# An RWKV attention and mixture-of-experts layer on one core: the last columns of each expert's gate and up packed into two full tiles, and the expert's steps reordered

## Chip, core and metric

The kernel runs on one core of one Trainium2 chip. A core has five engines that run their own instruction streams and meet at semaphores: TensorE (PE in the profile, its weight loads as PEld), VectorE (DVE), ScalarE (ACT), GpSimd (POOL) and SyncE (SP, which here only issues DMAs). The metric is the device time of one execution in microseconds (us), the median over the runs. Lower is better.

## What is computed

The layer takes x of shape (8, 512, 512), normalizes it, and adds an attention branch and a feed-forward branch to it. The change touches only the routed experts of the feed-forward branch, cut here to what matters:

```python
E, K, F = (32, 4, 352)          # experts, experts per token, hidden width
CAP = 256                       # rows of one expert
x = w_norm * (xf * rsqrt(mean(xf * xf) + eps))       # 4096 tokens, H = 512
probs = softmax(x @ w_router); w_topk, sel = top_k(probs, K)
buf = the rows of x sent to each expert, at most CAP   # (E, CAP, H)
g = einsum('ech,ehf->ecf', buf, w_gate)
u = einsum('ech,ehf->ecf', buf, w_up)
y = einsum('ecf,efh->ech', silu(g) * u, w_down)
out = y gathered back, weighted by w_topk, plus a shared expert
```

Everything is float32. The kernel reaches that precision on TensorE by splitting each operand into a high part (rounded to the format fp32r) and a low part (the rest), and adding three products: low weight with high row, high weight with low row, high with high (`PRODUCTS`).

## The kernel before

Three stages follow one another: the projections of the attention (`project_stage`, to about 430 us), the 32 experts (`expert_stage`, about 435 to 870 us) and the output stage (`output_stage`: shared expert, attention output, final sums). The change is inside the second.

**One expert** has 256 rows of 512 channels (KC = 4 chunks of 128). The hidden width of 352 is cut into three tiles `FT` of 128, 128 and 96 columns. On TensorE `one_expert` runs, for each tile, 12 gate products and 12 up products (3 part pairs x 4 chunks, line 1400), each with up to 128 weight columns held in the array and the 256 rows streamed: 72 products. Then `turn` (line 1392) transposes the 256 gathered rows of the next expert in 8 steps, and `down` (line 1427) makes 18 products of 512 columns.

**Around TensorE**, for each tile: ScalarE takes silu of the gate out of PSUM (`silu`, line 1256), VectorE multiplies it by up (`hidden`, line 1339), ScalarE rounds the result to its high part (`hidden_hi`, line 1262), VectorE makes the low part (`hidden_lo`, line 1344), and `down` waits for that (`h_lo`). Of the next expert, prepared meanwhile: ScalarE makes the high parts of the gate, up and down weights (`gate_hi` line 1234, `up_hi` line 1238, `down_hi` lines 1242 and 1244) and of the turned rows (`rows_hi`, line 1250). VectorE makes the low parts of up, down and rows (`up_lo` 1318, `down_lo` 1324 and 1326, `rows_lo` 1333). GpSimd makes the low part of the gate weights (`gate_lo`, line 1210) and issues the indirect DMAs that gather the rows of the expert after the next (line 1201). `keep_y` (line 1269) copies the expert's output out of PSUM. SyncE loads the weights two experts ahead.

Each engine's order is the order of the calls in its own `one_expert`; no scheduler changes it. An instruction that waits holds back all that stands behind it on its engine. Weights, inputs, rows and outputs have two buffers (`half`), `act_g` and `h` have one. Each tile has a PSUM bank of its own, gate in its first half and up in its second (`gu`).

## Time and profile before

| | us |
|---|---|
| median of 3 runs | 1688.76 |
| lowest and highest | 1687.11, 1691.56 |
| the profiled execution, device time | 1695.61 |
| its span, first to last instruction | 1693.8 |

The rows below come from the profiled execution, which is 6.85 us longer than the median. The page gives busy times and the chain of work that ended last, followed back from the end. A timeline lists the instructions of an engine by their start, like ones merged ("x12"), with the idle time before them in brackets. The busy time of a merged row runs to the end of its last instruction. Matmuls overlap: each is listed with 282 ns, while the next starts 118 ns later, so the pace is read from the starts of rows.

### The profile page before, as it was taken

To read this page: it belongs to the slowest core of one execution; us is meant where nothing else is said; L and a number is where in the kernel's file an instruction comes from. 1 tells how busy PE (TensorE), PEld (TensorE's weight loads), DVE (VectorE), ACT (ScalarE), POOL (GpSimd) and SP (SyncE) were. 2 spreads that over 40 slices of the span, in tenths; PEclk is the share of its full clock that TensorE was granted. 3 is DMA by queue.
4 is the path that set the end of the run, shared out by engine and by line. 5 is a ranking of instruction groups with operands and counts; after the bars stand their busy time and mean duration, and the time that the engine had idled before them with its cause. 6 is when DMAs were issued, how large, how long until landed. Compare 5 with 4: busy or idle time off the path is not lost.

```text
span 1693.8 us, 26093 instructions
## 1 busy us (share of the span) xinstructions
PE 1647.0 (97%) x8512; PEld 1402.2 (83%) x8512; DVE 1272.6 (75%) x1863; ACT 697.7 (41%) x1216; POOL 836.7 (49%) x691
## 2 busy tenths in 40 slices
PE   6999999998999999999998999999999999999999
PEld 4777888876999999999986788888788888888887
DVE  7989999997756555655579687676777768687776
ACT  5746555653766666666653212121221212112121
POOL 4587777774444444444457444251433525243351
PEclk9999999999999999999999999999999999999999
DMA  4544343424766666666687655454545343433431
GB/s 156 194 155 174 125 156 141 149 100 181 253 240 244 239 241 234 228 228 230 239 278 230 234 176 162 174 182 148 179 143 178 104 155 119 155 107 114 166 99 52
DMA packets 122420, 299.06 MB, mean 177 GB/s; under 512 B 19996, under 2 KB 31260, under 8 KB 117728
## 3 DMA queue, kind: packets, MB, share of 16 engines
q1 hardware_dynamic: 103104, 263.82, 43.6%
q0 software_dynamic: 18944, 33.66, 6.9%
q8 instruction: 44, 0.72, 0.2%
q10 hardware_dynamic: 288, 0.52, 0.1%
q14 instruction: 40, 0.33, 0.1%
HBM read 233.34 MB, written 81.35 MB: 186 GB/s over the span
## 4 chain that ended last, share of the span: by engine, by line
PE 74%; DVE 15%; issue 6%; ACT 2%; POOL 2%; another core or an unknown queue 0%; DMA 0%; DVEq 0%; POOLq 0%; ACTq 0%; SPq 0%
PE bank L2176 25%; PE bank L1400 16%; PE bank L2190 13%; PE bank L1427 8%; PE bank L2207 5%; PE bank L1024 4%; DVE mixf L719 3%; PE bank L1392 2%; DVE bank L687 1%; DVE st L667 1%; DVE mix L726 1%; DVE zT_lo L694 1%; DVE s_wg L2027 1%; PE bank L958 1%; DVE sr L740 1%
## 5 line engine op out<-in xcount | busy, mean ns | idle before, releaser
L1024 PE MATMUL bank<-mix,w 128*128 128x512 f32 x1488 | 353.7, 394 | 12.8 <-DVE ekv L735 7.6
L1024 PEld LDWEIGHTS bank<-mix,w 128*128 128x128 f32 x1488 | 277.0, 189 | 76.3 <-DVE ekv L735 5.8
L2176 PE MATMUL bank<-s_zT,s_wu 128*128 128x512 f32 x1056 | 256.7, 392 | 9.9 <-DVE bank L1932 9.9
L2190 PE MATMUL bank<-s_wd,s_h 128*128 128x512 f32 x1056 | 254.0, 390 | 1.1 <-DVE s_h L1938 1.1
L2176 PE MATMUL bank<-s_zT,s_wg 128*128 128x512 f32 x1056 | 253.7, 389 | 0.0
L2176 PEld LDWEIGHTS bank<-s_zT,s_wu 128*128 128x128 f32 x1056 | 199.5, 189 | 53.4 <-issue 11.9
L2190 PEld LDWEIGHTS bank<-s_wd,s_h 128*128 128x128 f32 x1056 | 198.4, 188 | 42.9 <-DVE s_h L1938 1.7
L2176 PEld LDWEIGHTS bank<-s_zT,s_wg 128*128 128x128 f32 x1056 | 198.2, 188 | 41.1
L1210 POOL TENSOR_TENSOR e_wg<-e_g_in,e_wg 128x1408 fp32r<-128x1408 f32 x31 | 100.7, 3249 | 212.6 <-ACT e_wg L1234 212.6
L1707 POOL DMA_INDIRECT s_picked<-y_rows,s_slot x128 | 140.6, 1099 | 78.3 <-DVE s_total L1988 39.1
L1816 ACT ACTIVATE s_act_g<-bank 128x512 f32<-128x512 f32 x88 | 52.5, 597 | 288.6 <-PE bank L2176 282.2
L1827 ACT ACTIVATE s_h<-bank 128x512 fp32r<-128x512 f32 x80 | 47.9, 598 | 263.5 <-DVE bank L1932 260.4
L1400 PE MATMUL bank<-e_xT,e_wu 128*128 128x256 f32 (+1 forms) x1152 | 152.1, 282 | 0.0
L1400 PE MATMUL bank<-e_xT,e_wg 128*128 128x256 f32 (+1 forms) x1152 | 152.1, 282 | 0.0
L1400 PEld LDWEIGHTS bank<-e_xT,e_wg 128*128 128x128 f32 (+1 forms) x1152 | 144.3, 180 | 2.6
L374 POOL TENSOR_TENSOR mix<-mixf,mix 128x512 fp32r<-128x512 f32 x88 | 118.4, 1358 | 50.3 <-ACT mix L498 49.3
L1400 PEld LDWEIGHTS bank<-e_xT,e_wu 128*128 128x128 f32 (+1 forms) x1152 | 142.1, 180 | 0.0
L1427 PE MATMUL bank<-e_wd,e_h 128*128 128x512 f32 (+1 forms) x576 | 140.1, 396 | 0.0
L1988 DVE SCALAR_TENSOR_TENSOR s_total<-s_picked,s_rec,s_total 128x512 f32<-128x512 f32 x128 | 136.9, 1070 | 3.4
L388 POOL DMA_INDIRECT slot_tokens<-token,slot x112 | 119.3, 1065 | 33.9 <-issue 24.3
L1427 PEld LDWEIGHTS bank<-e_wd,e_h 128*128 128x128 f32 (+1 forms) x576 | 106.2, 189 | 21.4
L1727 POOL TENSOR_TENSOR s_att<-s_gate,s_att 128x512 fp32r<-128x512 f32 x32 | 46.2, 1445 | 156.7 <-ACT s_att L1845 156.7
(188 smaller groups left out, 2489.3 us busy)
## 6 DMA issues: line engine op xcount, KB each, us to landing
s_wu<-wu_split SPq DMA_DIRECT2D x77, 512.0 KB
e_g_in<-in_w_gate SPq DMA_DIRECT2D x32, 704.0 KB
e_u_in<-in_w_up SPq DMA_DIRECT2D x32, 704.0 KB
e_d_in<-in_w_down SPq DMA_DIRECT2D x32, 512.0 KB
y_rows<-e_y SPq DMA_DIRECT2D x32, 512.0 KB, 2.9
s_zT<-zT_parts SPq DMA_DIRECT2D x16, 1024.0 KB, 6.8
zT_parts<-zT_hi SPq DMA_DIRECT2D x8, 1024.0 KB
zT_parts<-zT_lo SPq DMA_DIRECT2D x8, 1024.0 KB
```

What stands on the lines that cost most here:

```text
L374: pool.tensor_tensor(mix[:, i % 2, k, 1, :], mixf[:, k, :], mix[:, i % 2, k, 0, :].bitcast(F32), ALU.subtract).then_inc(lo_made, 1)
L388: pool.indirect_dma_start(d["slots"], bass.IndirectOffsetOnAxis(ap=slot[:, half, at:at + 1], axis=0), token[:, half, at // TOPK:at // TOPK ...
L1024: last = pe.matmul(pj[m][:], w[i][:, w_part, k, m * P:(m + 1) * P], mix[:, i % 2, k, x_part, :], start=(k == 0 and q == 0), stop=(k == KC ...
L1210: pool.tensor_tensor(wg[half][:, 1, :], g_in[half][:], wg[half][:, 0, :].bitcast(F32), ALU.subtract).then_inc(wg_lo, 1)
L1400: last = pe.matmul(gu[f][0:m, which, :], w[half][:, w_part, k * F + f0:k * F + f0 + m], xT[half][:, x_part, k, :], start=(q == 0 and k == ...
L1427: last = pe.matmul(yp[c][:], h[0:m, f, h_part, c * P:(c + 1) * P], wd[half][0:m, w_part, f, :], start=(f == 0 and q == 0), stop=(f == NF - ...
L1707: pool.indirect_dma_start(picked[:, k, :], None, d["y_flat"], bass.IndirectOffsetOnAxis(ap=slot[:, j * TOPK + k:j * TOPK + k + 1], axis=0) ...
L1816: act.activation(act_g[:, i, :], gp[:], ACT.Silu).then_inc(silu_made, 1)
L1988: dve.scalar_tensor_tensor(total[:, j, :], picked[:, k, :], rec[:, at:at + 1], total[:, j, :], ALU.mult, ALU.add).then_inc(picked_used, 1)
L2176: last = pe.matmul(into[:], w[:, w_part, k, :], zT[:, x_part, k, :], start=(q == 0 and k == 0), stop=(q == 2 and k == KC - 1))
L2190: last = pe.matmul(yp[j][:], h[:, i, h_part, j * P:(j + 1) * P], wd[f][:, w_part, :], start=(f == 0 and q == 0), stop=(f == NFS - 1 and q ...
L2207: last = pe.matmul(ob[j % 2][:], att[m][:, x_part, j * P:(j + 1) * P], wo[m][:, w_part, :], start=(m == 0 and q == 0), stop=(m == KC - 1 a ...
```

## The change

**Packing.** Gate and up together have 704 columns, which is five and a half tiles of 128, but took six (two of them with 96 columns). Now the gate weights are loaded as `w_first`, 384 columns wide: the 352 of gate and behind them the last 32 of up. The third gate tile so has 128 columns (96 gate, 32 up) and still 12 products. Of up remain 256 columns in two whole tiles, and 64 columns (`UA`), whose high and low parts lie side by side in one tile of 128 columns (`wua`). That tile takes 4 products with the low rows and 4 with the high rows, 8 in place of 12 (`product_third`). An expert has 68 products. The host lays the two weight arrays out (`w_first`, `w_second`); their bytes are together the same as before.

**Putting it together.** The up values of the third tile now come in three pieces of bank 6. ScalarE copies two of them to an SBUF tile `third` (`keep_third`, two instructions), VectorE adds the third piece (one more instruction), and the multiplication of the third tile then takes both of its inputs from SBUF (`act_g` and `third`).

**Order.** The packed tile is the first of an expert, then tiles 0 and 1 (`ORDER`). TensorE turns the next rows between its second and last tile. ScalarE does `up_hi` of the next expert at the start and `gate_hi` after the first tile's silu and `keep_third` (before: `gate_hi` at the start, `up_hi` after the first silu); `rows_hi` stands ahead of the last tile's silu. VectorE does `up_lo` ahead of the first `hidden`, and `rows_lo` ahead of the last. `up_hi` and `up_lo` are two instructions each (256 and 1024 elements a row, before one of 1408). `gate_hi` and `gate_lo` have 1536 elements a row, before 1408.

```diff
-        def silu(e, f):
+        def silu(e, at):
+            f = ORDER[at]
...
+        def keep_third(e):
+            act.wait_ge(up_done, e * NF + 1)
+            wait(act, h_made, gated(e - 1, 0) if not isinstance(e, int) or e else 0)
+            act.activation(third[0:UA, :], gu[2][UA:2 * UA, 1, :], ACT.Copy)
+            act.activation(third[UA:UA + UB, :], gu[2][P - UB:P, 0, :], ACT.Copy).then_inc(silu_made, 1)
...
             if more:
+                up_hi(e + 1, 1 - half, other)
+            silu(e, 0)
+            keep_third(e)
+            if more:
                 gate_hi(e + 1, 1 - half, other)
-            silu(e, 0)
-            if more:
-                up_hi(e + 1, 1 - half, other)
...
-        def hidden(e, f):
+        def hidden(e, at):
+            f = ORDER[at]
             m = FT[f][1]
-            dve.wait_ge(silu_made, e * NF + f + 1)
-            dve.tensor_tensor(act_g[0:m, f, :], act_g[0:m, f, :], gu[f][0:m, 1, :], ALU.mult).then_inc(h_made, 1)
+            dve.wait_ge(silu_made, gated(e, at))
+            if at == 0:
+                dve.tensor_tensor(third[0:UA, :], third[0:UA, :], gu[f][0:UA, 1, :], ALU.add).then_inc(h_made, 1)
+                dve.wait_ge(h_made, e * GATES + 1)
+            up = gu[f][0:m, 1, :] if at else third[0:m, :]
+            dve.tensor_tensor(act_g[0:m, f, :], act_g[0:m, f, :], up, ALU.mult).then_inc(h_made, 1)
...
+        def product_third(half):
+            for x_part in (1, 0):
+                for k in range(KC):
+                    last = pe.matmul(gu[NF - 1][:, 1, :], wua[half][:, k].rearrange("p q f -> p (q f)"),
+                                     xT[half][:, x_part, k, :], start=(x_part == 1 and k == 0),
+                                     stop=(x_part == 0 and k == KC - 1))
+            return last
...
         def one_expert(e, half, more, uses):
-            for f in range(NF):
-                up_gate(e, half, f)
+            up_gate(e, half, 0)
+            up_gate(e, half, 1)
             if more:
                 turn(e + 1, 1 - half, uses + half)
+            up_gate(e, half, 2)
             down(e, half)
```

ScalarE in the last but one expert, before, from the high part of the gate weights to the first of the turned rows (`e_wg1`, `e_wu1` are the next expert's weights, `e_act_g` takes silu, `e_h` the rounded hidden values):

```order
L1234 ACTIVATE e_wg1_120<-e_g_in1_126 128x1408 [waits e_y_done,e_g_loaded1]
L1256 ACTIVATE e_act_g_135<-bank6 128x256 [waits e_h_lo,e_up_done]
L1238 ACTIVATE e_wu1_122<-e_u_in1_128 128x1408 [waits e_u_loaded1]
L1262 ACTIVATE e_h_136<-e_act_g_135 128x256 [waits e_y_done,e_h_made]
L1256 ACTIVATE e_act_g_135<-bank0 128x256 [waits e_h_lo,e_up_done]
L1262 ACTIVATE e_h_136<-e_act_g_135 128x256 [waits e_y_done,e_h_made]
L1256 ACTIVATE e_act_g_135<-bank1 96x256 [waits e_h_lo,e_up_done]
L1262 ACTIVATE e_h_136<-e_act_g_135 96x256 [waits e_y_done,e_h_made]
L1250 ACTIVATE e_xT1_134<-bank4,keep_const_51 128x256 [waits e_turned]
```

And now, in the same place:

```order
L1256 ACTIVATE e_wua1_124<-e_u_in1_130 128x4x64 [waits e_y_done,e_u_loaded1]
L1257 ACTIVATE e_wu1_122<-e_u_in1_130 128x1024
L1276 ACTIVATE e_act_g_137<-bank6 96x256 [waits e_h_lo,e_up_done]
L1282 ACTIVATE e_third_139<-bank6 64x256 [waits e_h_made,e_up_done]
L1283 ACTIVATE e_third_139<-bank6 32x256
L1251 ACTIVATE e_wg1_120<-e_g_in1_128 128x1536 [waits e_y_done,e_g_loaded1]
L1290 ACTIVATE e_h_138<-e_act_g_137 96x256 [waits e_y_done,e_h_made]
L1276 ACTIVATE e_act_g_137<-bank0 128x256 [waits e_h_lo,e_up_done]
L1290 ACTIVATE e_h_138<-e_act_g_137 128x256 [waits e_y_done,e_h_made]
L1269 ACTIVATE e_xT1_136<-bank4,keep_const_51 128x256 [waits e_turned]
```

The conversion of the gate weights (`e_wg1`), which releases GpSimd, stood ahead of the first silu. Now it stands directly ahead of the first rounding of hidden values (`e_h`). The turned rows (line 1269, four instructions) moved ahead of the last silu, which follows them.

VectorE in the same expert, before (the first row multiplies silu by up, `e_h` rows make low parts, `e_xT1` rows the low parts of the next rows):

```order
L1339 TENSOR_TENSOR e_act_g_135<-e_act_g_135,bank6 128x256 [waits e_silu_made]
L1318 TENSOR_TENSOR e_wu1_122<-e_u_in1_128,e_wu1_122 128x1408 [waits e_wu_hi]
L1344 TENSOR_TENSOR e_h_136<-e_act_g_135,e_h_136 128x256 [waits e_h_hi]
L1339 TENSOR_TENSOR e_act_g_135<-e_act_g_135,bank0 128x256 [waits e_silu_made]
L1344 TENSOR_TENSOR e_h_136<-e_act_g_135,e_h_136 128x256 [waits e_h_hi]
L1339 TENSOR_TENSOR e_act_g_135<-e_act_g_135,bank1 96x256 [waits e_silu_made]
L1344 TENSOR_TENSOR e_h_136<-e_act_g_135,e_h_136 96x256 [waits e_h_hi]
L1333 SCALAR_TENSOR_TENSOR e_xT1_134<-bank4,keep_const_51,e_xT1_134 128x256 [waits e_x_hi] x2
L1333 SCALAR_TENSOR_TENSOR e_xT1_134<-bank5,keep_const_51,e_xT1_134 128x256 [waits e_x_hi] x2
```

And now:

```order
L1348 TENSOR_TENSOR e_wua1_124<-e_u_in1_130,e_wua1_124 128x4x64 [waits e_wu_hi]
L1349 TENSOR_TENSOR e_wu1_122<-e_u_in1_130,e_wu1_122 128x1024
L1372 TENSOR_TENSOR e_third_139<-e_third_139,bank6 64x256 [waits e_silu_made]
L1375 TENSOR_TENSOR e_act_g_137<-e_act_g_137,e_third_139 96x256 [waits e_h_made]
L1381 TENSOR_TENSOR e_h_138<-e_act_g_137,e_h_138 96x256 [waits e_h_hi]
L1375 TENSOR_TENSOR e_act_g_137<-e_act_g_137,bank0 128x256 [waits e_silu_made]
L1381 TENSOR_TENSOR e_h_138<-e_act_g_137,e_h_138 128x256 [waits e_h_hi]
L1364 SCALAR_TENSOR_TENSOR e_xT1_136<-bank4,keep_const_51,e_xT1_136 128x256 [waits e_x_hi] x2
L1364 SCALAR_TENSOR_TENSOR e_xT1_136<-bank5,keep_const_51,e_xT1_136 128x256 [waits e_x_hi] x2
L1375 TENSOR_TENSOR e_act_g_137<-e_act_g_137,bank1 128x256 [waits e_silu_made]
L1381 TENSOR_TENSOR e_h_138<-e_act_g_137,e_h_138 128x256 [waits e_h_hi]
```

The low parts of the up weights moved ahead of the first multiplication, which became an addition and a multiplication. The low parts of the rows moved ahead of the last tile's multiplication.

## Rows read from the trace of the kernel before

**Rows 1.** page: the chain that ended last, shares by engine and line

```profile
PE 74%; DVE 15%; issue 6%; ACT 2%; POOL 2%; another core or an unknown queue 0%; DMA 0%; DVEq 0%; POOLq 0%; ACTq 0%; SPq 0%
PE bank L2176 25%; PE bank L1400 16%; PE bank L2190 13%; PE bank L1427 8%; PE bank L2207 5%; PE bank L1024 4%; DVE mixf L719 3%; PE bank L1392 2%; DVE bank L687 1%; DVE st L667 1%; DVE mix L726 1%; DVE zT_lo L694 1%; DVE s_wg L2027 1%; PE b
```

**Rows 2.** chain of waits, one expert of the steady loop: start us, us, what

```profile
693.67 8.53 PE bank L1400 x72
702.20 0.95 PE bank L1392 x8
703.15 4.14 PE bank L1427 x18
```

**Rows 3.** TensorE timeline, one expert: start us, us, engine, line, op, out<-in, count

```profile
693.51 1.58 PE L1400 MATMUL bank<-e_xT,e_wg 128*128 128x256 f32 x12
...
697.77 1.58 PE L1400 MATMUL bank<-e_xT,e_wu 128*128 128x256 f32 x12
699.19 1.58 PE L1400 MATMUL bank<-e_xT,e_wg 128*96 128x256 f32 x12
...
702.91 4.38 PE L1427 MATMUL bank<-e_wd,e_h 128*128 128x512 f32 x18
707.13 1.58 PE L1400 MATMUL bank<-e_xT,e_wg 128*128 128x256 f32 x12
```

**Rows 4.** groups by shape, 475.75 to 843.33: weight loads of 128, 96 columns

```profile
L1400 PEld LDWEIGHTS bank<-e_xT,e_wg 128*128 128x128 f32 x648 | 82.3, 188 | 2.2
...
L1400 PEld LDWEIGHTS bank<-e_xT,e_wg 128*96 128x96 f32 x324 | 39.5, 163 | 0.0
```

**Rows 5.** ScalarE timeline, the same expert; brackets: idle before, releaser

```profile
694.20 1.38 ACT L1234 ACTIVATE e_wg<-e_g_in 128x1408 fp32r<-128x1408 f32 x1
696.63 0.39 ACT L1256 ACTIVATE e_act_g<-bank 128x256 f32<-128x256 f32 x1 [1.05 <-PE bank L1400]
...
698.18 0.40 ACT L1262 ACTIVATE e_h<-e_act_g 128x256 fp32r<-128x256 f32 x1
...
703.50 1.53 ACT L1250 ACTIVATE e_xT<-bank,keep_const 128x256 fp32r<-128x256 f32 x4
704.93 1.06 ACT L1242 ACTIVATE e_wd<-e_d_in 128x1024 fp32r<-128x1024 f32 x1
```

**Rows 6.** GpSimd timeline: the first expert, then the one at 693.51

```profile
436.89 3.65 POOL L1210 TENSOR_TENSOR e_wg<-e_g_in,e_wg 128x1408 fp32r<-128x1408 f32 x1 [9.72 <-ACT e_wg L1234]
...
695.66 3.24 POOL L1210 TENSOR_TENSOR e_wg<-e_g_in,e_wg 128x1408 fp32r<-128x1408 f32 x1 [6.81 <-ACT e_wg L1234]
```

**Rows 7.** VectorE timeline: the first expert, then the one at 693.51

```profile
436.23 1.22 DVE L1324 TENSOR_TENSOR e_wd<-e_d_in,e_wd 128x1024 fp32r<-128x1024 f32 x1
437.37 3.72 DVE L1326 TENSOR_TENSOR e_wd<-e_d_in,e_wd 96x512 fp32r<-96x512 f32 x1
...
697.05 0.42 DVE L1339 TENSOR_TENSOR e_act_g<-e_act_g,bank 128x256 f32<-128x256 f32 x1 [2.31 <-ACT e_act_g L1256]
698.32 2.06 DVE L1318 TENSOR_TENSOR e_wu<-e_u_in,e_wu 128x1408 fp32r<-128x1408 f32 x1 [0.85 <-ACT e_wu L1238]
...
704.35 1.66 DVE L1333 SCALAR_TENSOR_TENSOR e_xT<-bank,keep_const,e_xT 128x256 fp32r<-128x256 f32 x4 [0.30 <-ACT e_xT L1250]
```

**Rows 8.** lines 1318, 1326 and 1344: duration ns, min/median/max

```profile
L1318 DVE TENSOR_TENSOR e_wu<-e_u_in,e_wu x32: 1610/2133/2194, 428.2 to 848.1; 128x1408 fp32r<-128x1408 f32 x32
...
L1326 DVE TENSOR_TENSOR e_wd<-e_d_in,e_wd x32: 678/681/3724, 437.4 to 857.4; 96x512 fp32r<-96x512 f32 x32
...
L1344 DVE TENSOR_TENSOR e_h<-e_act_g,e_h x96: 408/422/866, 443.0 to 867.0; 128x256 fp32r<-128x256 f32 x64, 96x256 fp32r<-96x256 f32 x32
```

**Rows 9.** ScalarE timeline, the first expert: the table load ahead of its first silu

```profile
436.83 1.28 ACT L1256 ACT_TABLE_LOAD   x1
```

**Rows 10.** windows: us; busy PE, PEld, DVE, ACT, POOL; clock, DMA share, GB/s

```profile
404.00:420.00 16.00, 10.89 (x52) 8.50 (x53) 12.30 (x23) 3.33 (x6) 4.44 (x4) 0.89 0.41 157
...
888.00:904.00 16.00, 13.25 (x59) 10.67 (x58) 15.23 (x11) 4.65 (x8) 12.21 (x11) 1.00 0.79 247
```

More of the change, by code:

```diff
@@ L1118, in expert_stage @@
     h = at("e_h", [P, NF, 2, CAP], 214, F32R)
[L1119 removed]
+    third = at("e_third", [P, CAP], 24)
+    y = [at("e_y0", [P, NCT, C], 308), at("e_y1", [P, NCT, C], 120)]
     xt = bank[4:6]
[L1122 removed]
+    gu = [bank[i][:].rearrange("p (w s) -> p w s", w=2) for i in (0, 1, 6)]
     yp = [bank[7], bank[2]]
@@ L1284, in one_expert @@
             hidden_hi(e, 1)
+            if more:
+                rows_hi(e + 1, 1 - half)
             silu(e, 2)
@@ L1349, in one_expert @@
                 make_index(e + 2, half, uses + 1)
-            hidden(e, 0)
             if more:
                 up_lo(e + 1, 1 - half)
-            else:
+            hidden(e, 0)
+            if not more:
                 output_early[0]()
@@ L1359, in one_expert @@
             hidden_lo(e, 1)
+            if more:
+                rows_lo(e + 1, 1 - half)
             hidden(e, 2)
@@ L1403, in product, with gate_weight, up_weight, up_gate @@
             return last
-        def up_gate(e, half, f):
-            if f == 0:
+        def product_third(half):
[5 more added lines that the diff above has]
+            return last
+        def gate_weight(half, part, k, f):
+            return wg[half][:, part, k, f * P:(f + 1) * P]
+        def up_weight(half, part, k, f):
+            return wu[half][:, part, k * WHOLE + f * P:k * WHOLE + (f + 1) * P]
+        def up_gate(e, half, at):
+            f = ORDER[at]
+            if at == 0:
                 pe.wait_ge(x_lo, (e + 1) * KC)
                 pe.wait_ge(wg_lo, e + 1)
-            wait(pe, h_made, (e - 1) * NF + f + 1)
-            if f and isinstance(e, int) and e == 0:
-                pe.wait_ge(shared["gate_made"], B * KC - 4 + f)
-            product(e, half, f, 0, wg)
-            if f == 0:
+            wait(pe, h_made, gated(e - 1, at) if not isinstance(e, int) or e else 0)
+            if at and isinstance(e, int) and e == 0:
+                pe.wait_ge(shared["gate_made"], B * KC - 4 + at)
+            product(e, half, f, 0, gate_weight)
+            if at == 0:
                 pe.wait_ge(wu_lo, e + 1)
-            product(e, half, f, 1, wu).then_inc(up_done, 1)
+            (product(e, half, f, 1, up_weight) if at else product_third(half)).then_inc(up_done, 1)
         def down(e, half):
@@ L1427, in down @@
                         last = pe.matmul(yp[c][:], h[0:m, f, h_part, c * P:(c + 1) * P], wd[half][0:m, w_part, f, :],
-                                         start=(f == 0 and q == 0), stop=(f == NF - 1 and q == 2))
-                    if f == NF - 1:
+                                         start=(at == 0 and q == 0), stop=(at == NF - 1 and q == 2))
+                    if at == NF - 1:
                         last.then_inc(y_done, 1)
         def one_expert(e, half, more, uses):
-            for f in range(NF):
-                up_gate(e, half, f)
+            up_gate(e, half, 0)
+            up_gate(e, half, 1)
             if more:
                 turn(e + 1, 1 - half, uses + half)
+            up_gate(e, half, 2)
             down(e, half)
@@ L2379 @@
         give(name, np.asarray(inputs["L0_attn_" + name]).T)
-    for name in ("w_norm", "w_gate", "w_up", "w_down", "sw_gate", "sw_up", "sw_down"):
+    for name in ("w_norm", "w_down", "sw_gate", "sw_up", "sw_down"):
         give(name, inputs["L0_ffn_" + name])
+    up = np.asarray(inputs["L0_ffn_w_up"])
+    give("w_first", np.concatenate([np.asarray(inputs["L0_ffn_w_gate"]), up[:, :, F - UB:]], axis=2))
+    up = up.reshape(E, P, KC, F)
+    give("w_second", np.concatenate([up[:, :, :, 0:WHOLE].reshape(E, P, KC * WHOLE),
+                                     up[:, :, :, WHOLE:F - UB].reshape(E, P, KC * UA)], axis=2))
     give("const", constants(inputs))
```

60 lines of the change are left out of this document (36 added, 24 removed).

## The prediction

> **What bounds the kernel now.** I read three views in this order. The page's chain says that TensorE carries 74% of what ended last, and the lines of the experts (1400, 1427, 1392) 26% [rows 1]. The chain in order of time says more: one expert is 72 products, 8 turns and 18 down products with nothing between them, 8.53 + 0.95 + 4.14 = 13.62 us, and so it goes for all 32 [rows 2]. The first gate products of two experts start 13.62 us apart, too [rows 3]. So in this stage no wait counts at present, and a product less is time won, as long as the other engines keep up. The third view is therefore the timelines of the others over one expert [rows 5 to 7]. There two things are to be seen. They have idle time but run in a chain (silu, multiply, round, low part) whose end TensorE needs. And GpSimd's low part of the gate weights, 3.24 us, ends some 0.6 us after VectorE began the up weights [rows 6, 7].
>
> **A wait that the rows show.** VectorE's line 1318 takes 1.61 us at its shortest but 2.06 here [rows 7, 8]. GpSimd ended at 698.90, VectorE at 700.38, 1.48 later. In the first expert line 1326 took 3.72 us in place of 0.68; GpSimd had begun at 436.89 and ended at 440.54, VectorE began at 437.37 and ended at 441.09 [rows 6 to 8]. Both read two inputs from SBUF, and both end their own duration less 0.13 us after GpSimd does: they stand still while GpSimd computes. Line 1339, with one input in PSUM, ran inside GpSimd's instruction at 697.05 in its usual 0.42 [rows 7]. The low part of the hidden values (line 1344) reads two SBUF inputs as well; one of 96 took 0.87 in place of 0.42 [rows 8].
>
> This is a rule of the Trainium skill that speaks against the change (SBUF — State Buffer, "SBUF: two separate sides"): VectorE instructions with two SBUF inputs and GpSimd instructions share a port pair that the first one locks for its whole length. By it line 1344 waits out all of GpSimd's instruction; were the pair shared by bandwidth instead, it would take about 0.5 us and the change would win what TensorE saves. The rows agree with the lock.
>
> **TensorE's part.** 12 products start 1.42 us apart, whether of 128 or of 96 columns [rows 3], so widening costs nothing there. Four products less are 4 x 0.118 = 0.47 us an expert, 15.2 us over 32.
>
> A second rule weighs against that (TensorE: Matmul & The Clock Gate, "LDWEIGHTS"): a weight load takes time by its columns. The trace has it, 188 ns for 128 and 163 for 96 [rows 4], but under products that start 118 ns apart in both cases it is hidden.
>
> **The others, step by step.** Times are from an expert's first gate product (693.51 in the rows).
> ScalarE gets to the next expert's weights at 0.69, as before [rows 5]. The up weights' high part is now two instructions, 0.41 (256 elements) and 1.06 (1024), ending at 2.05 with their overlap of 0.1. VectorE's low parts, 0.41 and 1.22 [rows 7], end at 3.63. The packed tile's 20 products end at 2.37; the silu came 0.28 after the products (696.63 against 693.51 + 2.84) and so starts at 2.65. Silu and the two new copies, 0.39 each as the silu and with that overlap, end at 3.60. The gate weights' high part then takes 1.38 plus 128 elements at 0.83 ns (from 1.38 and 1.06 for 1408 and 1024), from 3.50 to 4.99. GpSimd followed 0.08 later and does again: from 5.07, for 3.24 x 1536/1408 = 3.53 us, to **8.60**.
> VectorE's new addition and the multiplication, 0.42 each, end at 4.50, before GpSimd starts. ScalarE rounds the first hidden values behind the gate weights, 4.89 to 5.29. Now VectorE wants its low part at 5.32, and GpSimd has been running for 0.25 us. It always has: in ScalarE's order the rounding stands directly behind the instruction that releases GpSimd. So it ends at 8.60 + 0.42 - 0.13 = **8.89**, in place of 5.74.
> Behind it stand on VectorE the second tile's multiplication (to 9.23), on which ScalarE's rounding waits (to 9.66), and behind that on ScalarE the four high parts of the rows, 1.53 (to 11.09), and the last silu (to 11.38). The rows' low parts start 0.85 after the high parts [rows 5, 7], at 10.41, and end at 12.07. Then come the last multiplication (12.41), rounding (12.84) and low part (**13.28**).
> TensorE is ready for the last third of the down products at 8.06 + 0.95 + 12 x 0.234 (18 take 4.22 [rows 3]) = 11.82. It waits until 13.4 and ends six products later, at **14.82**. The expert takes 1.20 us more than now, and not 0.47 less. Without the lock the same chain ends near 11.0, 0.8 us before TensorE needs it; the cover that the packing relies on is there but smaller than 3.15 us.
>
> **What costs nothing.** The added copies, the addition and the split instructions lie in the numbers above; alone they would be covered by those 0.8 us. SyncE's loads are as many bytes and are issued an expert ahead; the up weights are wanted some 3 us earlier, and ScalarE's rows show no wait for a DMA [rows 5]. On GpSimd the gathers stand behind its long instruction and start at 8.6 instead of 5.4, while the turn that needs them moves to 5.2 of the next expert: 11.4 us for issue and landing remain. TensorE's clock: the granted clock was 1.00 in a stretch with 2.75 us idle in 16, and 0.89 in one with 5.11 [rows 10]. A wait of 1.6 us in 14.8 is nearer to the first, so no term.
>
> **Ends.** In the first expert ScalarE must load the silu table, 1.28 us [rows 9], now behind the longer up conversion. GpSimd is released some 0.7 us later than in the loop, so this expert takes 1.9 more. The last one prepares no successor, has no such wait, and is 0.47 shorter.
>
> **Sum.** 30 x 1.20 + 1.9 - 0.5 = +37.4 us. Against the profiled execution, 1695.61 + 37.4 = 1733.0. That one stands 6.85 above the median, and 1688.76 + 37.4 = **1726**.
>
> **Bounds.** If GpSimd's duration did not grow with the elements (3.24), an expert is 0.29 us shorter, 9 us in all. The new copies have no row of their own; silu takes 0.39 and rounding 0.40 [rows 5]. With 0.1 to 0.15 more for each, GpSimd starts up to 0.3 later: 9 us more. TensorE's restart may take 0.1 to 0.2 more, 3 to 6 us. The output stage starts later as a whole; I give it 4 us either way. So 1712 to 1745.
>
> **Rivals.**
> A, all hidden: VectorE's low part gets through, and TensorE runs 68 products without a gap. 1688.8 - 15.2 = 1674. The point from which it decides: if GpSimd's instruction ends by 7.0 nothing waits, and by 7.4 the expert is as long as now; it would have to last 2.3 us, not 3.5. For it speaks that the pace of 118 ns is firm and that line 1344 itself was seen in this conflict once only. Against it: two other lines stopped in full. 0.07.
> B, the multiplication is caught as well: both of its inputs are now in SBUF. If the copies or the up weights come 0.57 us later than I reckon, it begins inside GpSimd's instruction. Then multiplication, rounding and low part follow 8.6 one after the other, 0.87 more an expert, 27 in all: 1753. 0.06.
> C, the wider weight loads show: 20 products with 25 ns more [rows 4] are 0.5 us an expert, 16 in all. In my forecast TensorE's wait swallows it; together with A it gives 1690, no change. It is what the Trainium skill's rule on weight loads (TensorE: Matmul & The Clock Gate) would do here if they were not hidden. 0.02.
> That the change doesn't save products can't be; in the forecast the saving only never shows, since TensorE waits longer.
>
> **Chances.** Forecast 0.85, A 0.07, B 0.06, C 0.02. Faster by over 0.3% (what a measurement can tell from no change) 0.07, within it 0.02, slower 0.91. The range leaves out A, C and most of B, and holds the forecast with its bounds.
>
> **What would show it.** In the new profile: an expert of some 14.8 us; in each a wait of TensorE of about 1.6 us ahead of the last six down products, put down to VectorE's low part; the first low part (96 rows) near 3.5 us and the others near 0.42; GpSimd's instruction near 3.53, begun some 5.1 us into the expert. It is wrong if that low part takes 0.42 (A), if the first multiplication takes over 3 us (B), or if products start more than 118 ns apart (C).

## The result and the profile after

The changed kernel takes 1738.84 us (median of 4 runs, 1736.48 to 1740.18), the kernel before, measured beside it, 1687.93 (4 runs, 1686.82 to 1691.56). The ratio is 1.0296 [1.0277, 1.0316]: slower by 50.9 us. Predicted were 1726 and a range of 1712 to 1745. The profiled execution took 1738.85 us, its span is 1737.0.

The chain that ended last, on the page of after. Before, TensorE carried 74% of it [rows 1]:

```profile
PE 55%; DVE 19%; issue 15%; ACT 9%; POOL 2%; ACTq 0%; DMA 0%; DVEq 0%; POOLq 0%; SPq 0%
PE bank L2230 24%; PE bank L2244 13%; PE bank L2261 5%; PE bank L1028 5%; DVE mixf L723 3%; PE bank L1480 3%; PE bank L1437 3%; DVE e_xT L1364 2%; PE bank L1446 2%; ACT e_wg L1251 2%; ACT e_h L1290 1%; DVE e_h L1381 1%; ACT e_xT L1269 1%; DVE bank L691 1%; DVE st L671 1%
```

The experts' own products (lines 1437, 1446, 1480) fell to 8% of the chain; before, lines 1400 and 1427 had 24% [rows 1]. TensorE's timeline over one expert shows why (start us, us, engine, line, op, out<-in, count, idle before and its releaser):

```profile
703.72 1.59 PE L1437 MATMUL bank<-e_xT,e_wg 128*128 128x256 f32 x12
705.16 1.12 PE L1446 MATMUL bank<-e_xT,e_wua 128*128 128x256 f32 x8
706.12 1.60 PE L1437 MATMUL bank<-e_xT,e_wg 128*128 128x256 f32 x12
...
709.88 1.68 PE L1437 MATMUL bank<-e_xT,e_wg 128*128 128x256 f32 x12
711.40 1.60 PE L1437 MATMUL bank<-e_xT,e_wu 128*128 128x256 f32 x12
712.92 3.04 PE L1480 MATMUL bank<-e_wd,e_h 96*128 96x512 f32 x12
717.35 1.65 PE L1480 MATMUL bank<-e_wd,e_h 128*128 128x512 f32 x6 [1.39 <-DVE e_h L1381]
718.84 1.35 PE L1437 MATMUL bank<-e_xT,e_wg 128*128 128x256 f32 x10
```

The packed tile is there (12 and 8 products), and so is the wait: 1.39 us ahead of the last six down products, put down to VectorE's low part of the hidden values. (The listing counts idle time from the listed end of a product, 0.39 us after its start, where the next could start after 0.23.) The expert takes 718.84 - 703.72 = 15.12 us, against 13.62 before [rows 3].

GpSimd and VectorE in the same expert (same columns):

```profile
709.08 3.50 POOL L1227 TENSOR_TENSOR e_wg<-e_g_in,e_wg 128x1536 fp32r<-128x1536 f32 x1 [9.24 <-ACT e_wg L1251]
```

```profile
707.97 0.42 DVE L1375 TENSOR_TENSOR e_act_g<-e_act_g,e_third 96x256 f32<-96x256 f32 x1
709.34 3.52 DVE L1381 TENSOR_TENSOR e_h<-e_act_g,e_h 96x256 fp32r<-96x256 f32 x1 [0.95 <-ACT e_h L1290]
712.79 0.41 DVE L1375 TENSOR_TENSOR e_act_g<-e_act_g,bank 128x256 f32<-128x256 f32 x1
713.68 0.42 DVE L1381 TENSOR_TENSOR e_h<-e_act_g,e_h 128x256 fp32r<-128x256 f32 x1 [0.48 <-ACT e_h L1290]
714.40 1.66 DVE L1364 SCALAR_TENSOR_TENSOR e_xT<-bank,keep_const,e_xT 128x256 fp32r<-128x256 f32 x4 [0.30 <-ACT e_xT L1269]
715.98 0.41 DVE L1375 TENSOR_TENSOR e_act_g<-e_act_g,bank 128x256 f32<-128x256 f32 x1
716.87 0.43 DVE L1381 TENSOR_TENSOR e_h<-e_act_g,e_h 128x256 fp32r<-128x256 f32 x1 [0.48 <-ACT e_h L1290]
```

GpSimd runs from 709.08 to 712.58. Of VectorE's three low parts (line 1381) two take 0.42 and 0.43, and the one that begins 0.26 us into GpSimd's instruction takes 3.52, ending 0.28 after it. A multiplication with an input in PSUM ran inside GpSimd's instruction in the kernel before, in its usual 0.42 [rows 7]. This low part has both inputs in SBUF. ScalarE in the same expert:

```profile
706.32 0.38 ACT L1276 ACTIVATE e_act_g<-bank 96x256 f32<-96x256 f32 x1 [0.54 <-PE bank L1446]
706.72 0.38 ACT L1282 ACTIVATE e_third<-bank 64x256 f32<-64x256 f32 x1
707.12 0.38 ACT L1283 ACTIVATE e_third<-bank 32x256 f32<-32x256 f32 x1
707.52 1.49 ACT L1251 ACTIVATE e_wg<-e_g_in 128x1536 fp32r<-128x1536 f32 x1
708.91 0.40 ACT L1290 ACTIVATE e_h<-e_act_g 96x256 fp32r<-96x256 f32 x1
```

The last two overlap by 0.10 (707.52 + 1.49 against 708.91). The two copies and the gate conversion start 0.40 apart although each copy takes 0.38: no overlap.

**Where the time went, by stage.** The first gate product of the first expert and that of the last lie 422.21 us apart before (31 experts) and 470.91 after: +48.7. From the last expert's first product to the end it is 836.85 before and 836.29 after: -0.56, the packing's saving in the expert that prepares no successor. The profiled execution of after entered the stage 4.9 us earlier (429.85 against 434.74), in code the change doesn't touch. The spans so differ by 48.7 - 0.56 - 4.9 = 43.2.

### The profile page after: what moved, and what is told of

Same layout as the page of the kernel before. It is cut to its first block, busy times and chain, and to the rows that moved or that the text cites. A ratio compares the mean times of both kernels' runs of the same rounds, so it can differ in the third digit from the quotient of the medians.

```text
span 1737.0 us, 26324 instructions
## 1 busy us (share of the span) xinstructions
PE 1651.2 (95%) x8384; PEld 1390.0 (80%) x8384; DVE 1363.8 (79%) x1927; ACT 725.8 (42%) x1312; POOL 810.6 (47%) x691
## 4 chain that ended last, share of the span: by engine, by line
PE 55%; DVE 19%; issue 15%; ACT 9%; POOL 2%; ACTq 0%; DMA 0%; DVEq 0%; POOLq 0%; SPq 0%
PE bank L2230 24%; PE bank L2244 13%; PE bank L2261 5%; PE bank L1028 5%; DVE mixf L723 3%; PE bank L1480 3%; PE bank L1437 3%; DVE e_xT L1364 2%; PE bank L1446 2%; ACT e_wg L1251 2%; ACT e_h L1290 1%; DVE e_h L1381 1%; ACT e_xT L1269 1%; DVE bank L691 1%; DVE st L671 1%
## 5 line engine op out<-in xcount | busy, mean ns | idle before, releaser
L1227 POOL TENSOR_TENSOR e_wg<-e_g_in,e_wg 128x1536 fp32r<-128x1536 f32 x31 | 108.5, 3501 | 292.6 <-ACT e_wg L1251 292.6
L2230 PEld LDWEIGHTS bank<-s_zT,s_wu 128*128 128x128 f32 x1056 | 198.7, 189 | 54.6 <-issue 13.4
L1480 PE MATMUL bank<-e_wd,e_h 128*128 128x512 f32 (+1 forms) x576 | 149.7, 404 | 44.0 <-DVE e_h L1381 44.0
L1381 DVE TENSOR_TENSOR e_h<-e_act_g,e_h 128x256 fp32r<-128x256 f32 (+1 forms) x96 | 138.4, 1442 | 60.1 <-ACT e_h L1290 53.8
L1437 PE MATMUL bank<-e_xT,e_wg 128*128 128x256 f32 x1152 | 156.1, 285 | 0.0
L1437 PEld LDWEIGHTS bank<-e_xT,e_wg 128*128 128x128 f32 x1152 | 147.0, 191 | 2.7
L502 ACT ACTIVATE mix<-mixf 128x512 fp32r<-128x512 f32 x128 | 78.4, 631 | 106.0 <-DVE mixf L723 94.7
```

The costliest lines, as they stand in the source:

```text
L1227: pool.tensor_tensor(wg[half][:, 1].rearrange("p k f -> p (k f)"), g_in[half][:], wg[half][:, 0].rearrange("p k f -> p (k f)").bitcast(F32 ...
L1381: dve.tensor_tensor(h[0:m, f, 1, :], act_g[0:m, f, :], h[0:m, f, 0, :].bitcast(F32), ALU.subtract).then_inc(h_lo, 1)
L1437: last = pe.matmul(gu[f][:, which, :], w(half, w_part, k, f), xT[half][:, x_part, k, :], start=(q == 0 and k == 0), stop=(q == 2 and k == ...
L1480: last = pe.matmul(yp[c][:], h[0:m, f, h_part, c * P:(c + 1) * P], wd[half][0:m, w_part, f, :], start=(at == 0 and q == 0), stop=(at == NF ...
L2230: last = pe.matmul(into[:], w[:, w_part, k, :], zT[:, x_part, k, :], start=(q == 0 and k == 0), stop=(q == 2 and k == KC - 1))
```

## Experiments

The theory is that of the prediction: one lock, at one place. GpSimd's subtraction keeps VectorE's first low part out of SBUF, and the rows that now stand ahead of the last silu hand this on to TensorE. The rival: the new order has made the chain behind the second tile too long by itself, and the lock is only its loudest part. All edits below are to the changed kernel unless said otherwise. "Stage" is the distance between first and last expert as above.

| run | stage us | expert us | TensorE idle in an expert | median, ratio to before |
|---|---|---|---|---|
| before | 422.21 | 13.62 | none | |
| after | 470.91 | 15.13, 15.21 in turn | 1.4 | 1738.8, 1.0296 |
| e1 gate first | 412.05 | 13.25 | none | 1684.1, 0.9967 [0.9952, 0.9982] |
| e2 low part zeroed | 410.85 | 13.25 | none | 1686.95, one run |
| e3 gate after second | 422.50 | 13.57, 13.65 | 0.02, 0.10 | 1694.1, 1.0013 [1.0, 1.0026] |
| e4 rows at end | 429.91 | 13.81, 13.90 | 0.13 | 1702.4, 1.0064 [1.0043, 1.0085] |
| e5 copies in place | 466.37 | 14.98, 15.05 | 1.4 | 1735.2, one run |
| e6 packed last | 433.11 | 13.95 | 0.43 | 1700.1, 1.0067 [1.0053, 1.0082] |
| e7 gate first, rows at end | 411.07 | 13.26 | none | 1680.1, 0.9954 [0.9942, 0.9966] |
| e8 order only | 443.49 | 14.26, 14.33 | 0.36, 0.43 | 1709.1, 1.0120 [1.0105, 1.0134] |
| e9 second copy cut | 468.15 | 15.04, 15.12 | 1.4 | 1737.2, one run |
| e10 1152 columns | 445.30 | 14.30, 14.38 | 0.74, 0.83 | 1713.9, one run |
| e11 768 columns | 419.67 | 13.47, 13.55 | none shown | 1690.9, one run |

The kernel before took 1691.4 us (median of 20 runs) beside e1 to e4, 1688.1 (11 runs) beside e5 to e8, and 1687.3 (one run) beside e9 to e11. Where there is one run only, the stage and the expert decide, not the time. The idle time is less than what an expert loses, since it is counted from the listed ends and leaves out products that are only late or slower around a wait: in after 1.4 of 15.12 - 13.25 = 1.87. e2, e5, e9, e10 and e11 leave out or replace part of the computation; they serve as tests only.

**e1: the gate weights first, the up weights after the copies; their low parts last.**

```diff
             if more:
-                up_hi(e + 1, 1 - half, other)
+                gate_hi(e + 1, 1 - half, other)
             silu(e, 0)
             keep_third(e)
             if more:
-                gate_hi(e + 1, 1 - half, other)
+                up_hi(e + 1, 1 - half, other)
...
-            if more:
-                up_lo(e + 1, 1 - half)
             hidden(e, 0)
...
             if more:
+                up_lo(e + 1, 1 - half)
                 down_lo(e + 1, 1 - half)
```

> The changed kernel (68 products, packed tile first, rows turned before the last tile), but ScalarE makes the gate weights' high part at the expert's start, as in the kernel before, and the up weights' after the packed tile's silu and copies; VectorE makes the up weights' low part only after the last tile's low part. GpSimd then runs from about 2.3 to 5.8 us of the expert, before the first low part of hidden values is asked for. Theory (GpSimd's instruction locks VectorE out at that one place): the first low part takes 0.42 us, TensorE has no gap, an expert takes 13.2 to 13.3 us, 1673 to 1680 in all. Rival (the chain has become too long by the added copies, the addition and the earlier rows, whatever GpSimd does): the same work is in it, so an expert stays at 14.8 to 15.2 and the time at 1725 to 1739.

Measured: 13.25 us an expert and no wait of TensorE. GpSimd and VectorE in one expert of e1:

```profile
606.66 3.51 POOL L1227 TENSOR_TENSOR e_wg<-e_g_in,e_wg 128x1536 fp32r<-128x1536 f32 x1 [7.37 <-ACT e_wg L1251]
```

```profile
608.28 0.41 DVE L1372 TENSOR_TENSOR e_third<-e_third,bank 64x256 f32<-64x256 f32 x1 [2.38 <-ACT e_third L1283]
608.73 1.72 DVE L1375 TENSOR_TENSOR e_act_g<-e_act_g,e_third 96x256 f32<-96x256 f32 x1
610.93 0.42 DVE L1381 TENSOR_TENSOR e_h<-e_act_g,e_h 96x256 fp32r<-96x256 f32 x1 [0.48 <-ACT e_h L1290]
```

The lock hasn't gone. It now catches the multiplication with two SBUF inputs, but only for GpSimd's last 1.4 us, and at a point that TensorE doesn't need for long. The low part takes 0.42. With the same rows ahead of the last silu nothing waits, so the rival falls as far as the order goes. The whole kernel, at 1684.1, is slower than the 1673 to 1680 that I expected (the part on the rivals below takes this up).

**e2: the same instruction, mostly without its reading.**

```diff
-            pool.tensor_tensor(wg[half][:, 1].rearrange("p k f -> p (k f)"), g_in[half][:], wg[half][:, 0].rearrange("p k f -> p (k f)").bitcast(F32),
-                               ALU.subtract).then_inc(wg_lo, 1)
+            low = wg[half][:, 1].rearrange("p k f -> p (k f)")
+            high = wg[half][:, 0].rearrange("p k f -> p (k f)")
+            pool.tensor_tensor(low[:, 0:P], g_in[half][:, 0:P], high[:, 0:P].bitcast(F32), ALU.subtract)
+            pool.memset(low[:, P:].bitcast(F32), 0.0).then_inc(wg_lo, 1)
```

> The changed kernel, its order untouched; GpSimd computes the low part of only 128 of the 1536 gate columns a row and fills the other 1408 with zeros, so the gate's low parts are missing from the result. GpSimd's work of 3.5 us becomes about 1.5 us, and most of it reads nothing. Theory: if a fill holds the lock, the first low part of hidden values takes about 1.9 us, else 0.42; in both cases TensorE has no gap, an expert takes 13.2 to 13.3 us, 1673 to 1681 in all. Rival (chain too long by itself): nothing on ScalarE, VectorE or TensorE has changed, so 15.1 us an expert and 1735 to 1740.

GpSimd, then VectorE, in one expert of e2:

```profile
610.19 0.46 POOL L1229 TENSOR_TENSOR e_wg<-e_g_in,e_wg 128x128 fp32r<-128x128 f32 x1 [9.24 <-ACT e_wg L1253]
610.59 1.27 POOL L1230 MEMSET e_wg<- 128x1408 f32 x1
```

```profile
610.44 0.48 DVE L1383 TENSOR_TENSOR e_h<-e_act_g,e_h 96x256 fp32r<-96x256 f32 x1 [0.95 <-ACT e_h L1292]
```

Order and place are those of the changed kernel; GpSimd's work is shorter, 1.67 us in all, and reads SBUF only for its first 0.46. The whole loss goes, and the expert comes to the 13.25 of e1. (The kernel took 1686.95 in one run, where I expected 1673 to 1681.) The low part ended at 610.92, inside the fill (610.59 to 611.86) and 0.27 after the subtraction. It had been waiting since before the fill began, though, so this alone doesn't show that a fill would let VectorE in. The kernel before has that case, in its output stage (GpSimd, then VectorE):

```profile
876.39 1.81 POOL L1758 MEMSET s_picked<- 128x2048 f32 x1
```

```profile
876.66 0.68 DVE L1978 TENSOR_TENSOR s_gate<-s_gate,s_ek 128x512 f32<-128x512 f32 x1
```

A multiplication with two SBUF inputs begins 0.27 us into a fill and takes 0.68, its median over the 32 of that line. That is how the Trainium skill has it (SBUF — State Buffer, "SBUF: two separate sides": two SBUF inputs on VectorE contend only with a GpSimd operation that reads SBUF), and this trace agrees.

**e10 and e11: the dose.** As e2, with 1152 and 768 columns subtracted. Here e11 is shown against e2.

```diff
-            pool.tensor_tensor(low[:, 0:P], g_in[half][:, 0:P], high[:, 0:P].bitcast(F32), ALU.subtract)
-            pool.memset(low[:, P:].bitcast(F32), 0.0).then_inc(wg_lo, 1)
+            pool.tensor_tensor(low[:, 0:768], g_in[half][:, 0:768], high[:, 0:768].bitcast(F32), ALU.subtract)
+            pool.memset(low[:, 768:].bitcast(F32), 0.0).then_inc(wg_lo, 1)
```

> As e2_gate_low_zeroed, but GpSimd subtracts 1152 of the 1536 columns of the gate weights' low part and fills the other 384 with zeros; that leaves 384 columns of the low parts out of the computation. Theory (what stops the first low part is GpSimd's subtraction for its whole length, and each us of it beyond a slack is a us of TensorE's wait): from 0.46 us for 128 columns and 3.50 for 1536 the subtraction takes about 2.67, the first low part 2.67 or so in place of 3.52, and an expert 15.12 - 0.83 = 14.29 us. Rival (a part of the wait has another cause, such as the chain behind the second tile, that would show only once the lock is shorter): an expert of more than 14.4 us.

> The same with 768 columns subtracted and 768 filled with zeros. The subtraction takes about 1.84 us. Theory: with no wait an expert is 13.25 us (e1, e2), 1.87 less than in the changed kernel, so the slack is used up at a subtraction of 3.50 - 1.87 = 1.63 us. At 1.84 a wait of about 0.2 us is left, and an expert takes 13.45. By the thresholds of the prediction (nothing waits up to an end at 7.0 of an expert, and 0.3 less now that the subtraction starts 0.3 later than forecast) it would be the same to 0.1. Rival as above: more than 13.6.

VectorE's first low part in e10, then in e11:

```profile
608.45 2.70 DVE L1383 TENSOR_TENSOR e_h<-e_act_g,e_h 96x256 fp32r<-96x256 f32 x1 [0.95 <-ACT e_h L1292]
```

```profile
612.09 1.86 DVE L1383 TENSOR_TENSOR e_h<-e_act_g,e_h 96x256 fp32r<-96x256 f32 x1 [0.95 <-ACT e_h L1292]
```

GpSimd's subtraction took 2.67 and 1.84 us, the low part 2.70 and 1.86, the expert 14.30 and 13.47 (the shorter of the two values). In both, as in after, the low part ends 0.28 after the subtraction. From 3.50 to 2.67 to 1.84 us of lock, the expert goes 15.12, 14.30, 13.47: 0.82 and 0.83 for 0.83 each time. So from 1.84 us up every us of lock is a us of the expert. On that slope e2's 13.25 would be reached at 1.84 - 0.22 = 1.6 us; this is an estimate, as no run lies between 0.46 and 1.84. Rows and last silu stay where the change put them in all of this, so the loss scales with the lock; what their place adds to it is for e4 to show.

**e3: the gate weights after the second rounding.**

```diff
             keep_third(e)
-            if more:
-                gate_hi(e + 1, 1 - half, other)
-            else:
+            if not more:
                 output_early[0]()
...
             if more:
+                gate_hi(e + 1, 1 - half, other)
                 rows_hi(e + 1, 1 - half)
```

> The changed kernel with one step moved: ScalarE makes the gate weights' high part behind the second tile's rounding in place of the first's. GpSimd then runs from about 8.5 to 12 us of the expert. Theory: the first two low parts are free; what meets GpSimd is the second's or the last's, late, and the rows' high parts start 1.4 us later: 13.7 us an expert by the same stepwise sum, 1685 to 1697 in all. Rival (chain too long by itself): no work is gone, 1725 to 1740.

Measured: 13.57 and 13.65 in turn, as long as before (13.62). The first low part is free (0.42), but the gate conversion of 1.5 us now stands ahead of the rows and the last silu. These are later for it, and GpSimd, released later, catches the last low part with its end: that one takes 0.64 in place of 0.43. So the saving of the packing is just used up. The ratio's interval begins at 1.0: no difference that this measurement can tell.

**e4: the turns, and the rows, after the last tile as before.**

```diff
             hidden_hi(e, 1)
-            if more:
-                rows_hi(e + 1, 1 - half)
             silu(e, 2)
             hidden_hi(e, 2)
             if more:
+                rows_hi(e + 1, 1 - half)
...
             up_gate(e, half, 1)
+            up_gate(e, half, 2)
             if more:
                 turn(e + 1, 1 - half, uses + half)
-            up_gate(e, half, 2)
```

(VectorE's `rows_lo` moves in the same way.)

> The changed kernel with the next rows back at the end of the expert on TensorE, ScalarE and VectorE (turned after the last tile, their parts made after the last tile's low part); the gate weights stay where the change put them, so GpSimd still blocks the first low part for 3.5 us. Theory: the lock is the same, but the last silu no longer stands behind four row instructions, so less of it reaches TensorE: 13.9 us an expert, 1690 to 1702 in all. Rival (the lock alone sets the loss, wherever the rows stand): 15.1 us and 1735 to 1740. Second rival (the rows' place alone sets it): no gap, 13.2 us and 1673 to 1680.

Measured: 13.81 and 13.90. The lock is as long (the first low part takes 3.53), yet 1.3 of the 1.5 us are gone. Against kernels with the rows in the same place and GpSimd out of the way of the low parts, the lock costs 15.12 - 13.25 = 1.87 with the rows ahead of the last silu (after against e2), and 13.81 - 13.26 = 0.55 with them at the end (e4 against e7). So lock and order cost this much only together: the lock delays the second tile's rounding, and in the new order the rows and the last silu queue behind it. Here the delay reaches TensorE by another way; what the listing shows as idle is 0.13 us ahead of the next expert's first product.

**e6 and e8: either half of the change alone.** e6 has the packing in the order of before (packed tile last, gate weights first, up weights after the first silu); e8 is the kernel before with the new order and nothing packed:

```diff
             if more:
-                gate_hi(e + 1, 1 - half, other)
+                up_hi(e + 1, 1 - half, other)
             silu(e, 0)
             if more:
-                up_hi(e + 1, 1 - half, other)
+                gate_hi(e + 1, 1 - half, other)
...
-            for f in range(NF):
-                up_gate(e, half, f)
+            up_gate(e, half, 0)
+            up_gate(e, half, 1)
             if more:
                 turn(e + 1, 1 - half, uses + half)
+            up_gate(e, half, 2)
```

(In e8 `rows_hi`, `rows_lo` and `up_lo` move as in the change, and `up_hi`, now at the start, waits for `y_done` as it does there.)

> The packing alone: 68 products, but tiles, weights and next rows in the order of the kernel before, so the packed tile is the last of an expert and its copies, addition and multiplication stand right before the last third of the down products. GpSimd works from 2.3 to 5.8 us, where VectorE makes the up weights' low part. Theory by the same stepwise sum: the first low part of hidden values waits behind the up weights' (held up by GpSimd), and the rows' parts end late: 13.8 to 13.9 us an expert against 13.62, so 4 to 9 us above the kernel before. Rival (the packing is free where the order is the old one): 13.2 us, 10 to 14 us below the kernel before.

> The kernel before with the change's order of steps and no packing: 72 products, tiles in their old order, up weights' high and low part at the start, gate weights' high part between the first silu and the first rounding, next rows turned between the second and the last tile. Theory: GpSimd's 3.24 us start 0.3 us before the first low part of hidden values, which takes 3.2 to 3.3 us; 14.3 to 14.4 us an expert, 20 to 25 us above the kernel before. Rival (the packed tile's copies, addition and multiplication make the loss): 13.62 us an expert, the kernel before's time.

Measured: the order alone costs 0.64 an expert, the packing alone 0.33, the two together 1.50. (e6 was expected 4 to 9 us above the kernel before and is 12 above, at 13.95 an expert for 13.8 to 13.9.) In e8 the lock sits where it does in after (3.25 us, GpSimd having 1408 columns), and TensorE waits for it at the same place:

```profile
605.30 3.25 DVE L1346 TENSOR_TENSOR e_h<-e_act_g,e_h 128x256 fp32r<-128x256 f32 x1 [0.98 <-ACT e_h L1263]
```

```profile
613.03 1.66 PE L1430 MATMUL bank<-e_wd,e_h 96*128 96x512 f32 x6 [0.35 <-DVE e_h L1346]
```

What packing adds to this chain can be read off. In e8 GpSimd starts 4.78 us into the expert (605.05 against TensorE's first gate product at 600.27), in after 5.36. That is 0.58 later: the two copies put the gate conversion 1.20 behind the silu in place of 0.28, the silu comes 0.44 sooner (2.60 for 3.04, as the packed tile has 20 products and not 24), and the conversion of 1536 columns takes 0.10 longer. And GpSimd runs for 3.50 in place of 3.22, because of the wider tile: 14.26 + 0.58 + 0.28 = 15.12. The products saved don't enter, since TensorE waits for the end of the chain anyway. In e6 the conflict is another: the low parts of the up weights wait for GpSimd (the short one took 1.67 and 1.75 in turn where 0.42 is usual), everything behind them is late, and TensorE idles 0.43 ahead of the next expert:

```profile
610.85 1.69 PE L1435 MATMUL bank<-e_xT,e_wg 128*128 128x256 f32 x12 [0.43 <-DVE e_xT L1363]
```

**e7: e1 and e4 together.** The edits of both, `up_lo` behind `rows_lo`.

> As the first experiment (packed tile first, gate weights' high part at the start, up weights' low part late), with the next rows turned after the last tile again and their parts made after the last tile's. No low part of hidden values meets GpSimd. Theory: no gap, and TensorE has one switch between products and turns less, which the first experiment showed as a first row of products 0.08 us longer behind the turns: 13.15 to 13.2 us an expert, 2 to 3 us below the first experiment, 0.5 to 0.7% below the kernel before. Rival (the rows' parts come too late for the next expert's first products): 13.4 us or more, 3 us or more above the first experiment.

Measured: 1680.1 us, ratio 0.9954 [0.9942, 0.9966], 13.26 an expert, no idle time, and the first expert takes 13.27. In e1 that one takes 14.45. In both the second half of `down_lo` is held up there by GpSimd, for 4.01 us, and the first low part of hidden values begins at 7.97 us; but e7's last low part ends at 10.96 and e1's, behind the rows, at 12.90. The place of the rows on TensorE, ScalarE and VectorE makes these 1.9 us. This is the best version found: the packing with the gate conversion left at the start. It missed the 13.15 to 13.2 that I expected by the slower pace of the products (below).

**e5 and e9: why the copies don't overlap.** e5 lets the first copy read partitions 0 to 63 and the second 64 to 95, where they also write; these are other up values than the product needs. e9, shown here, cuts e5's second copy in two along its columns.

```diff
-            act.activation(third[0:UA, :], gu[2][UA:2 * UA, 1, :], ACT.Copy)
-            act.activation(third[UA:UA + UB, :], gu[2][P - UB:P, 0, :], ACT.Copy).then_inc(silu_made, 1)
+            act.activation(third[0:UA, :], gu[2][0:UA, 1, :], ACT.Copy)
+            act.activation(third[UA:UA + UB, 0:P], gu[2][UA:UA + UB, 0, 0:P], ACT.Copy)
+            act.activation(third[UA:UA + UB, P:CAP], gu[2][UA:UA + UB, 0, P:CAP], ACT.Copy).then_inc(silu_made, 1)
```

> The changed kernel, but keep_third's two copies take other values of the same size from PSUM: partitions 0 to 63 and 64 to 95, where they also write, in place of 64 to 127 and 96 to 127. The packed tile's up values in the result are therefore wrong. In the changed kernel silu, the two copies and the gate weights' high part start 0.40 us apart, each after its predecessor has ended, where the silu before the change was followed after 0.28. Theory (the shift across partitions takes the overlap away): 0.28 to 0.30 apart now, GpSimd starts 0.3 us earlier, 14.8 to 14.9 us an expert and some 8 to 10 us less than the changed kernel. Rival (fewer than 128 partitions, or something else, takes it away): still 0.40 apart, 15.1 to 15.2 us an expert, the changed kernel's time within 3 us.

> The changed kernel with the copies of e5_copies_in_place, the second of them cut in two along its columns (partitions 64 to 95 both times, 128 columns each). As in e5, these copies read other partitions than the product needs, so the hidden values are not the right ones. Question: two successive ScalarE instructions overlap by about 0.1 us in the weights, rows and the first copy of e5, and not when the second starts at another partition. Theory (a change of the start partition ends the overlap): the second piece starts about 0.1 before the first piece ends, and the first piece (after the copy from partition 0) and the gate conversion (back at partition 0) start behind the end of what stands ahead of them. Rival (any instruction that starts at partition 64 does not overlap with its neighbours): the second piece too starts at or behind the end of the first. The expert takes 0.1 to 0.3 us more than in e5 (15.06), since ScalarE's queue ahead of the gate weights is longer by one short instruction.

ScalarE in e9:

```profile
613.93 0.38 ACT L1276 ACTIVATE e_act_g<-bank 96x256 f32<-96x256 f32 x1 [0.55 <-PE bank L1447]
614.21 0.36 ACT L1282 ACTIVATE e_third<-bank 64x256 f32<-64x256 f32 x1
614.58 0.27 ACT L1283 ACTIVATE e_third<-bank 32x128 f32<-32x128 f32 x1
614.76 0.25 ACT L1284 ACTIVATE e_third<-bank 32x128 f32<-32x128 f32 x1
615.04 1.49 ACT L1251 ACTIVATE e_wg<-e_g_in 128x1536 fp32r<-128x1536 f32 x1
```

The first copy, at partition 0 like the silu, starts 0.10 before the silu's end. The next is at partition 64 and waits for the first copy's end (614.21 + 0.36 = 614.57). The second piece, at 64 again, overlaps by 0.09. The gate conversion, back at 0, waits. It is the change of the start partition that costs 0.1 us, not the partition itself. In e5 I had expected 14.8 to 14.9 with all of the overlap back; it was 14.98 and 15.05, since only one of three starts came back. e9's expert is 0.06 to 0.07 longer than e5's, where I expected 0.1 to 0.3.

## Why the prediction was right, and where its size was off

**What bounds the kernel, and the lock.** Right. Predicted was that the first low part ends at 8.89 us of the expert in place of 5.74; it ends at 9.14. Everything behind it keeps the forecast order (predicted in brackets): second multiplication to 9.48 (9.23), rounding 9.93 (9.66), rows' high parts 11.38 (11.09), last silu 11.66 (11.38), last multiplication 12.67 (12.41), last low part 13.58 (13.28), TensorE again at 13.63 (13.4), next expert 15.12 (14.82). Its thresholds hold: GpSimd's end by 7.0 was to cost nothing, and by the slope of e10 and e11 it stops to cost at 5.36 + 1.63 = 6.99. An end by 7.4 was to make the expert as long as before, 13.62; on the same slope that is a lock of 1.84 + 0.15 = 2.0, and 5.36 + 2.0 = 7.4.

**The term that was too small: the two copies.** "0.39 each as the silu and with that overlap" is the term that was mis-sized. Silu, two copies and gate conversion start 0.40 apart, not 0.28, which is 0.35 in all. The silu itself came 0.05 sooner than forecast, so GpSimd starts at 5.36 and not at 5.07, and the whole chain shifts with it: 0.3 us an expert, 9 of the 13.5 us by which the forecast was short. The bounds had this very case ("0.1 to 0.15 more for each ... 9 us more"), from the argument that the copies have no row of their own. I took the end at which they behave like their neighbours. e9 shows what makes them differ.

**TensorE's part.** The saving is real and doesn't show, as forecast: in e1, e2 and e7 it does. It is 13.62 - 13.25 = 0.37 there, not 0.47. Away from a wait, twelve products start 1.44 us apart (703.72 and 705.16) in the packed kernels, 1.42 in before [rows 3] and in e8; over 68 products this is the missing 0.1. So the sign that was to stand for rival C (products more than 118 ns apart) appeared, at a fifth of C's price, but not by C's mechanism, wider tiles: before has 1.42 for 128 and for 96 columns alike, and in after the tiles that had 128 columns before run at 1.44 too (706.12 to 707.56). Why the pace differs is open.

**Ends, and the rest.** The first expert took 15.90, 2.3 over the 13.62 where 1.9 were predicted. Every second expert takes 0.08 more than the other (15.13, 15.21), 1.2 us in all. The difference is there in every kernel, before too: ScalarE's first silu starts 2.59 us into one expert and 2.67 into the next (3.04 and 3.12 in before), with TensorE's products at the same places. It costs time only where TensorE waits for the chain behind that silu, as in after, e3, e4, e5 and e8 to e11, and not in e1, e2, e6 or e7. Why the silu starts later is open. After the wait the six last products and the step to the next expert took 1.49 for a forecast 1.42. Together the stage and the last expert make 48.7 - 0.56 = 48.1 of the 50.9 us between the medians; the other 2.8 can't be placed from two profiled executions, and are within what I gave the output stage (4 either way).

**The rivals.** A (all hidden) fell by the 3.52 us of the low part in the changed kernel; it is what e1, e2 and e7 are. Its time was put at 1674; the real gain of a hidden packing, by the ratios of e1 and e7, is 5.6 to 7.8 us, not 15. A fifth of the products' saving goes to the pace; the stage is 10.2 us shorter in e1 and 11.1 in e7. In the one profiled execution of e7 the part behind the stage is 3.6 us longer than before (840.43 from the last expert's first product to the end, against 836.85), in that of e1 it is not (836.44). Over the kept traces that part lies between 835.8 and 841.8 us and doesn't follow the length of the stage, so single traces don't place the rest: where it goes is open. B (multiplication caught) didn't happen: it began at 707.97 and ended 0.69 before GpSimd's start, where I had 0.57. That 0.57 was the distance to the multiplication's end; to begin inside GpSimd's instruction, as B has it, it would have to come about 0.99 later, so B had less room than its text says. e1 shows that the multiplication can be caught (1.72 us) and what decides the price: not the lock, but whether TensorE needs what stands behind it.

## What to carry to other kernels

An instruction that releases a long GpSimd operation shouldn't stand directly ahead of one that feeds a VectorE instruction with two SBUF inputs on the critical chain. Look for each such pair in the order of the queues, and cost it at GpSimd's whole remaining duration, then subtract the slack behind it; put the release where VectorE next works from PSUM or waits anyway. A saving on the engine that bounds the kernel shrinks everyone else's cover by the same amount, so measure that cover first.

## What the runs showed of the hardware

- Two successive ScalarE instructions overlap by 0.09 to 0.11 us, unless the second starts at another partition than the first; then it starts 0.01 to 0.03 after the first one's end (e9, and the 0.40 spacing in after). The Trainium skill has such a rule for VectorE (VectorE: DVE Perf Modes, "Two Vector instructions with no wait between them": an instruction whose operands start in another quadrant of partitions is held until the earlier ones are done). ScalarE's starts shown of after and of e9 agree with it.
- GpSimd's fill doesn't keep VectorE out (0.68 us as usual, inside a fill of 1.81, in before), its subtraction does, for its whole length: 3.50, 2.67 and 1.84 us gave 3.52, 2.70 and 1.86, and each of these low parts ended 0.28 after it.
- The gate and up products start 120 ns apart on average (1.44 us for 12) in every kernel with the packed weights, and 118 (1.42) in before and e8, at a granted clock of 1.00 in either. Not explained.
